# Cross-attention on one core: the order of the first projections, who rounds the key weights, and the warming matmuls

## The reference

```python
Q = (query @ Wq.T + bq)        # query x: (8, 112, 256); 16 heads of 16
K = (key_value @ Wk.T + bk)    # context: (8, 375, 256)
V = (key_value @ Wv.T + bv)
scores = einsum('bhqd,bhkd->bhqk', Q, K) / sqrt(16)
context = einsum('bhqk,bhkd->bhqd', softmax(scores), V)
x = context @ W_o.T + b_o + query
return (x - mean(x)) / sqrt(var(x) + 1e-5) * gamma + beta
```

## Time and profile before

| | us |
|---|---|
| median of 3 runs | 149.48 |
| the three runs | 149.48, 149.32, 150.67 |
| the profiled execution's own time | 148.18 |
| its span (first to last instruction) | 146.4 |
| outside the span in that execution | 1.78 |
| PE busy / DVE busy / ACT busy / POOL busy | 132.2 / 94.6 / 88.9 / 82.4 |

### The profile page before, as it was taken

How to read it: one execution, slowest core, us unless ns; L and a number is a source line. 1 busy time by engine, 2 the same in 40 slices (tenths; PEclk the granted TensorE clock), 3 DMA queues, 4 the chain that set the end, 5 groups by cost and what they waited for, 6 DMA issues and landing times.

```text
span 146.4 us, 3925 instructions
## 1 busy us (share of the span) xinstructions
PE 132.2 (90%) x1479; PEld 116.1 (79%) x1479; DVE 94.6 (65%) x223; ACT 88.9 (61%) x180; POOL 82.4 (56%) x101
## 2 busy tenths in 40 slices
PE   5799999799999789698999999999999999999950
PEld 4599778589799668588898989898989888878620
DVE  3446798797857745467657776877687787521532
ACT  3637734648587826647586678665867566787410
POOL 8963998394429441300429998991247006597441
PEclk9999999999999999999999999999999999999996
DMA  4985895584039999670007104651071000011111
GB/s 117 352 312 180 241 343 174 196 250 173 4 83 226 283 238 252 216 239 23 8 0 262 56 6 129 197 204 29 24 263 53 16 26 4 4 36 34 36 31 31
DMA packets 15731, 19.59 MB, mean 134 GB/s; under 512 B 2544, under 2 KB 14896, under 8 KB 15712
## 3 DMA queue, kind: packets, MB, share of 16 engines
q1 hardware_dynamic: 14656, 17.36, 37.2%
q0 software_dynamic: 592, 1.70, 4.7%
q10 hardware_dynamic: 464, 0.28, 0.6%
HBM read 6.30 MB, written 0.92 MB: 49 GB/s over the span
## 4 chain that ended last, share of the span: by engine, by line
PE 65%; SPq 13%; DMA 12%; DVE 3%; issue 2%; ACT 2%; ACTq 1%; POOLq 0%; DVEq 0%
PE m_bank L860 15%; PE pv_bank L952 13%; PE st_bank L934 12%; PE mx_bank L901 11%; SPq L269 6%; SPq L321 5%; PE m_bank L983 4%; DMA q_stack<-shift 4%; DMA k_stack<-k_hl 3%; DMA c_raw<-ctxT 3%; PE m_bank L963 2%; PE mx_bank L934 2%; DMA q_stack<-q_hl 2%; DVE mx L717 1%; SPq L354 1%
## 5 line engine op out<-in xcount | busy, mean ns | idle before, releaser
L717 DVE TENSOR_REDUCE mx<-mx_bank 112x1 f32<-112x375 f32 x128 | 64.1, 541 | 24.5 <-PE mx_bank L901 24.2
L617 ACT ACTIVATE pw<-st_bank 125x448 f32<-125x448 f32 x86 | 45.5, 544 | 23.0 <-PE st_bank L934 22.6
L901 PE MATMUL mx_bank<-k_stack,q_stack 128*112 128x376 f32 x128 | 43.8, 354 | 3.2 <-DMA k_stack<-k_hl 1.7
L934 PE MATMUL st_bank<-q_stack,k_stack 128*125 128x224 f32 x172 | 35.0, 285 | 2.0 <-DMA q_stack<-shift 1.4
L934 PEld LDWEIGHTS st_bank<-q_stack,k_stack 128*125 128x125 f32 x172 | 28.6, 186 | 5.4 <-issue 2.0
L901 PEld LDWEIGHTS mx_bank<-k_stack,q_stack 128*112 128x112 f32 x128 | 22.2, 176 | 6.4 <-issue 1.9
L421 POOL TENSOR_TENSOR k_hl<-k_full,k_hl 128x376 fp32r<-128x376 f32 x10 | 10.0, 1005 | 21.6 <-ACT k_hl L538 21.6
L952 PE MATMUL pv_bank<-pw,v_sb 125*17 125x112 f32 x744 | 21.7, 260 | 0.0
L395 POOL TENSOR_TENSOR c_hl<-c_raw,c_hl 128x752 fp32r<-128x752 f32 x6 | 10.9, 1810 | 16.2 <-ACT c_hl L509 16.2
L860 PE MATMUL m_bank<-c_hl,w_hl 128*128 128x376 f32 x84 | 18.5, 362 | 1.1 <-ACT w_hl L501 0.8
L952 PEld LDWEIGHTS pv_bank<-pw,v_sb 125*17 125x17 f32 x744 | 16.6, 97 | 3.2 <-issue 1.9
(11 more groups left out here) (111 smaller groups left out, 171.5 us busy)
## 6 DMA issues: line engine op xcount, KB each, us to landing
k_stack<-k_hl SPq DMA_DIRECT2D x48, 188.0 KB, 2.5
c_raw<-ctxT SPq DMA_DIRECT2D x8, 375.0 KB, 4.1
q_stack<-q_hl SPq DMA_DIRECT2D x12, 112.0 KB, 2.3
q_stack<-q_hl SPq DMA_DIRECT2D x6, 168.0 KB, 3.4
x_space<-x_nat POOLq DMA_DIRECT2D x1, 896.0 KB, 11.0
out<-yo SPq DMA_DIRECT2D x8, 112.0 KB, 2.0
pw<-wT SPq DMA_DIRECT2D x2, 256.0 KB, 4.6
x_space<-xT SPq DMA_DIRECT2D x2, 224.0 KB, 5.5
```

The lines of the kernel that those rows point to most:

```text
L617: nc.scalar.activation(p_tile[0:KC, n % PR, :, :], st_of(n)[0:KC, 0:4 * Q].rearrange("p (j q) -> p j q", j=4), ACT.Exp, scale=float(DK) ** ...
L717: nc.vector.tensor_reduce(mx[b % 2][:, h % 2, q_pair(h // 2):q_pair(h // 2) + 1], mx_bank[n % MR][0:Q, 0:KV], axis=AX_X, op=ALU.max, negat ...
L901: nc.tensor.matmul(mx_bank[n % MR][0:Q, 0:KVP], q_stack[k][:, side, q_pair(h // 2), b - Q_STACKS[k][0], :], k_stack[b % 3][:, h // 2, :], ...
L934: last = nc.tensor.matmul(st_of(n)[0:KC, k * 2 * Q:(k + 1) * 2 * Q], k_stack[i % 3][:, 2 * g + k, c * KC:(c + 1) * KC], q_stack[qk][:, :, ...
```

## The change

- **W_K is rounded by DVE** (`wk_hi_part`, a `tensor_copy`), ahead of the lo part of context 0, while ACT rounds context 0. ACT no longer does it. The lo part of W_K is made in two halves (`wk_lo_part(t)`, 256 elements a partition each). Semaphores `wk_hi` and `wk_lo` are new; `W_ORDER` is gone.
- **K of batch 0 by products** (`k_project_first`): both halves t get the first product, then both the second, then t = 0 the third and t = 1 the third. The number of matmuls is the same, 12.
- **The second Q group in front of K of batch 1**: the two `q_project(1, t)` leave `EARLY_JOBS` and stand between V of batch 0 and K of batch 1 on PE; ACT and DVE do their Q parts in the same order, x 1 is rounded ahead of context 1 and is loaded ahead of it. Banks: Q of group 1 goes to the S banks and K of batch 1 to the M banks. The remaining `EARLY_JOBS` move up by one or two heads.
- **Stacking**: side 0 of group 1 is issued by SP ahead of K of batch 1 (`stack_q(sp, 1, 0)`), side 1 by POOL behind its memset of the stack (`stack_q(pool, 1, 1)`).
- **DVE's early order**: `q_lo_part(1, t)` stands ahead of the early heads, `k_lo_part(2, 1)` behind head 15 and no longer behind head 16, `k_lo_part(2, 0)` behind head 13, the first half of the shift behind head 8 and no longer behind head 9.
- **ACT's early order**: both `v_part(1, n)` go ahead of rounding x 2, and x 3 is rounded behind the issue of the shift's half.
- **Warming**: one more float32 matmul, of 128 columns, behind the four.

```diff
--- before.py
+++ after.py
@@ -60,15 +60,14 @@
 
 
 EARLY_HEADS = 16
-EARLY_JOBS = {1: ("Q", 1, 0), 3: ("Q", 1, 1), 5: ("V", 1, 0), 7: ("V", 1, 1), 9: ("MT", 0, 0), 10: ("V", 1, 2),
-              13: ("K", 2, 0), 15: ("K", 2, 1)}
+EARLY_JOBS = {1: ("V", 1, 0), 3: ("V", 1, 1), 5: ("V", 1, 2), 8: ("MT", 0, 0), 11: ("K", 2, 0), 13: ("K", 2, 1)}
 FIRST_JOBS = {1: (("MT", 0, 1),), 5: (("Q", 2, 0),), 6: (("Q", 2, 1),)}
 
 
-S0_JOBS = [("Q", 0, 0), ("K", 1, 0), ("V", 1, 0), ("MT", 0, 0)]
-S1_JOBS = [("Q", 0, 1), ("K", 1, 1), ("V", 1, 1)]
-M0_JOBS = [("K", 0, 0), ("V", 0, 0), ("Q", 1, 0), ("K", 2, 0), ("V", 2, 0), ("Q", 2, 0), ("K", 3, 0)]
-M1_JOBS = [("K", 0, 1), ("V", 0, 1), ("Q", 1, 1), ("K", 2, 1), ("MT", 0, 1), ("V", 2, 1), ("Q", 2, 1), ("MT", 1), ("K", 3, 1)]
+S0_JOBS = [("Q", 0, 0), ("Q", 1, 0), ("V", 1, 0), ("MT", 0, 0)]
+S1_JOBS = [("Q", 0, 1), ("Q", 1, 1), ("V", 1, 1)]
+M0_JOBS = [("K", 0, 0), ("V", 0, 0), ("K", 1, 0), ("K", 2, 0), ("V", 2, 0), ("Q", 2, 0), ("K", 3, 0)]
+M1_JOBS = [("K", 0, 1), ("V", 0, 1), ("K", 1, 1), ("K", 2, 1), ("MT", 0, 1), ("V", 2, 1), ("Q", 2, 1), ("MT", 1), ("K", 3, 1)]
 for _i in range(1, B - V_AHEAD):
     if _i == 2:
         M1_JOBS.append(("BIAS",))
@@ -170,7 +169,7 @@
         shift_in = [sem(f"shift_in{i}") for i in range(2)]
         half_in = [sem(f"half_in{t}") for t in range(2)]
         stored = [sem(f"stored{i}") for i in range(2)]
-        w_hi, w_lo, wv_lo, x_hi, x_lo = sem("w_hi"), sem("w_lo"), sem("wv_lo"), sem("x_hi"), sem("x_lo")
+        wk_hi, wk_lo, w_hi, w_lo, wv_lo, x_hi, x_lo = sem("wk_hi"), sem("wk_lo"), sem("w_hi"), sem("w_lo"), sem("wv_lo"), sem("x_hi"), sem("x_lo")
         c_hi, c_lo, c_pad = sem("c_hi"), sem("c_lo"), sem("c_pad")
         ident_clear, ident_ready = sem("ident_clear"), sem("ident_ready")
         pv_clear = sem("pv_clear")
@@ -194,7 +193,6 @@
         last_scaled, last_ready = sem("last_scaled"), sem("last_ready")
         rstd_ready, y_ready, y_scaled, yo_ready = sem("rstd_ready"), sem("y_ready"), sem("y_scaled"), sem("yo_ready")
 
-        W_ORDER = (1, 0, 2)
         WIDE = UNITS * (B - 2) + 4
         LATE = WIDE + 2
         SINGLE = UNITS * (B - 2) + NC
@@ -302,8 +300,8 @@
             load_x(0)
             load_w(0)
             load_w(2)
+            load_x(1)
             load_context(1)
-            load_x(1)
             load_x(2)
             load_x(3)
             load_context(2)
@@ -334,12 +332,11 @@
             stack_q(sp, 0, 0)
             stack_k(0, 1)
             load_context(3)
+            stack_q(sp, 1, 0)
             for t in range(2):
                 stack_k(1, t)
-            stack_q(sp, 1, 0)
             sp.wait_ge(shift_ready, 1)
             stack_shift_half(sp, 0, 1)
-            stack_q(sp, 1, 1)
             for t in range(2):
                 stack_k(2, t)
             load_context(4)
@@ -379,7 +376,7 @@
             nc.gpsimd.memset(k_stack[0][:].bitcast(F32), 1.0).then_inc(k_ones[0], 1)
             nc.gpsimd.memset(k_stack[1][:].bitcast(F32), 1.0).then_inc(k_ones[1], 1)
             at = slice(2 * D, 3 * D)
-            pool.wait_ge(w_hi, W_ORDER.index(2) + 1)
+            pool.wait_ge(w_hi, 2)
             nc.gpsimd.tensor_tensor(w_hl[1][:, :, at], w_raw[:, :, at], w_hl[0][:, :, at].bitcast(F32),
                                     op=ALU.subtract).then_inc(wv_lo, 1)
             nc.gpsimd.memset(ident[:, :], 0.0).then_inc(ident_clear, 1)
@@ -389,6 +386,7 @@
             nc.gpsimd.memset(minus_half[:, :], -0.5).then_inc(half_ready, 1)
             stack_q(pool, 0, 1)
             nc.gpsimd.memset(q_stack[1][:].bitcast(F32), 0.0).then_inc(q_clear[1], 1)
+            stack_q(pool, 1, 1)
 
             def context_lo(b):
                 pool.wait_ge(c_hi, b + 1)
@@ -550,7 +548,6 @@
                                ).then_inc(v_ready, 1)
 
             context_hi(0)
-            w_hi_part(1)
             x_hi_part(0)
             w_hi_part(0)
             w_hi_part(2)
@@ -559,26 +556,27 @@
                 k_hi_part(0, t)
             for t in range(2):
                 q_hi_part(0, t)
+            x_hi_part(1)
             context_hi(1)
             for n in range(2):
                 v_part(0, n)
-            x_hi_part(1)
+            for t in range(2):
+                q_hi_part(1, t)
             for t in range(2):
                 k_hi_part(1, t)
             context_hi(2)
-            for t in range(2):
-                q_hi_part(1, t)
-            v_part(1, 0)
-            for k in range(2, NQ):
-                x_hi_part(k)
+            for n in range(2):
+                v_part(1, n)
+            x_hi_part(2)
 
             act.wait_ge(shift_hi, 1)
             stack_shift_half(act, 0, 0)
-            v_part(1, 1)
+            x_hi_part(3)
             for t in range(2):
                 k_hi_part(2, t)
             context_hi(3)
-            act.wait_ge(w_lo, 2)
+            act.wait_ge(wk_lo, 2)
+            act.wait_ge(w_lo, 1)
             act.wait_ge(wv_lo, 1)
 
             def take_o(b):
@@ -661,10 +659,20 @@
                 nc.vector.tensor_tensor(x_hl[:, 1, :, at], x_raw[:, :, at], x_hl[:, 0, :, at].bitcast(F32),
                                         op=ALU.subtract).then_inc(x_lo, 1)
 
-            def w_lo_part(k):
-                dve.wait_ge(w_hi, W_ORDER.index(k) + 1)
-                at = slice(k * D, (k + 1) * D)
+            def wk_hi_part():
+                dve.wait_ge(w_in[1], 16)
+                nc.vector.tensor_copy(w_hl[0][:, :, D:2 * D], w_raw[:, :, D:2 * D]).then_inc(wk_hi, 1)
+
+            def wk_lo_part(t):
+
+                dve.wait_ge(wk_hi, 1)
+                at = slice(D + t * PART, D + (t + 1) * PART)
                 nc.vector.tensor_tensor(w_hl[1][:, :, at], w_raw[:, :, at], w_hl[0][:, :, at].bitcast(F32),
+                                        op=ALU.subtract).then_inc(wk_lo, 1)
+
+            def wq_lo_part():
+                dve.wait_ge(w_hi, 1)
+                nc.vector.tensor_tensor(w_hl[1][:, :, 0:D], w_raw[:, :, 0:D], w_hl[0][:, :, 0:D].bitcast(F32),
                                         op=ALU.subtract).then_inc(w_lo, 1)
 
             def context_lo(b):
@@ -695,19 +703,23 @@
                 dve.wait_ge(const_in, 48)
                 nc.vector.tensor_tensor(bo_rows[:, :], src[0:Q, 0:D], bo_rows[:, :], op=ALU.add).then_inc(bias_ready, 1)
 
+            wk_hi_part()
             context_lo(0)
-            w_lo_part(1)
+            for t in range(2):
+                wk_lo_part(t)
             x_lo_part(0)
-            w_lo_part(0)
+            wq_lo_part()
             dve.wait_ge(bqk_in, 16)
             for t in range(2):
                 k_lo_part(0, t)
             for t in range(2):
                 q_lo_part(0, t)
+            x_lo_part(1)
             context_lo(1)
             for i in range(1, VR):
                 nc.vector.memset(v_sb[i][:, :, :, DK:VW], 1.0).then_inc(v_ones, 1)
-            x_lo_part(1)
+            for t in range(2):
+                q_lo_part(1, t)
             for t in range(2):
                 k_lo_part(1, t)
 
@@ -761,20 +773,18 @@
 
             for n in range(EARLY_HEADS):
                 head_max(n)
-                if n - 4 in range(2):
-                    q_lo_part(1, n - 4)
-                if n == H // 2 + 1:
+                if n == H // 2:
                     take_shift_half(0)
-                if n == 14:
+                if n == 13:
                     k_lo_part(2, 0)
+                if n == 15:
+                    k_lo_part(2, 1)
             for i in range(B):
                 for u in range(UNITS):
                     heads = MAX_HEADS[UNITS * i + u]
                     for n in heads[:1]:
                         head_max(n)
 
-                    if u == 0 and i == 0:
-                        k_lo_part(2, 1)
                     if u == 1 and i == 0:
                         take_shift_half(1)
                     if u in (6, 7) and i == 0:
@@ -861,20 +871,34 @@
                                                 stop=(k == len(PRODUCTS) - 1 and e == EC - 1))
                 return last
 
-            def w_split(k):
-                return W_ORDER.index(k) + 1
-
             def q_project(k, t):
                 dst, full = claim("Q", k, t)
                 project(dst[:, 0:q_width(k)], lambda a, e: w_hl[a][:, e, t * PART:(t + 1) * PART],
                         lambda a, e: x_hl[:, a, e, q_rows(k)],
-                        ((x_hi, k + 1), (w_hi, w_split(0))), (x_lo, k + 1), (w_lo, w_split(0))).then_inc(full, 1)
+                        ((x_hi, k + 1), (w_hi, 1)), (x_lo, k + 1), (w_lo, 1)).then_inc(full, 1)
 
             def k_project(b, t):
                 dst, full = claim("K", b, t)
                 project(dst[:, 0:KVP], lambda a, e: w_hl[a][:, e, D + t * PART:D + (t + 1) * PART],
                         lambda a, e: c_hl[b % 2][:, a, e, :],
-                        ((c_hi, b + 1), (w_hi, w_split(1))), (c_lo, b + 1), (w_lo, w_split(1))).then_inc(full, 1)
```

(28 more changed lines are left out.)

## The result

The changed kernel is slower. Its median is 152.04 us (151.02 to 154.16, 4 runs), that of the kernel before in the same call 149.40 us (148.69 to 150.67, 4 runs); the ratio is 1.030 (95%: 1.021 to 1.039). The forecast was 147.7 us.

The account below looks back on a forecast made before the run. PE was taken as the bound from 61 us on, the front before it as SP's DMA queue and DVE's list. 149.48 - 1.2 (front) - 0.6 (later clock rise in timed runs) = 147.7 us; range 146.4 to 149.5.

Parts of the forecast that it names:

- W_K is then rounded at 5.8: Start of PE: W_K lands at about 5.13, DVE's rounding takes at most 0.68 us, so K starts at 6.0, 0.4 earlier.
- The clock: PE, K of batch 0: hole closed, rise to 2.4 GHz at 7.7 (5.6 to 9.9), K ending 1.44 us earlier.
- rival 3: Front: Q ahead delays K(1) and DVE's list, with the clock's rise at 10.5 or later; 150.4 us, chance 0.07.
- rival 1: Front: the clock rises at once, moving the mark by 2.0 us; 146.7 us, chance 0.20.
- 0.6 us for a later rise in the timed runs: Timed runs above the profiled one: part is a later clock rise, which the change removes; 0.6 us, between 0 and 1.3.
- Q of group 1 ahead of K(1): PE's front: 1.46 us more ahead of K(1), cancelled by the earlier K; DVE's first maximum stays at 17.3.
- DVE's list: DVE to the shift's second-half rounding at 29.62: -0.72 (Q parts), -0.62 (gap), +0.15 (V jobs), -1.2 us in all.
- Queues: SP and POOL in the front: nine SP issues of 0.64 us put the shift's row at about 22.6, before 23.31.
- It's covered by the K part on DVE: PE's unit 0, behind the shift's row, moves from 26.85 to 26.2; DVE's K part hides it.
- Both of these hang on the maxima and shifts that come before them, so an earlier front moves them along: PE's DMA waits before 61 us, 1.7 us for batch 3's K stack and 1.4 for a shift, move with the front.
- rival 2: Warming fails (rise at 9.9, 0.2 us left) or the gain is lost behind 40 us (some 0.5 left); 149.1 us, chance 0.28.
- Slower: Whole kernel: chance 0.03 of being slower beyond 1%, above 151.0 us; 0.44 within 1%, 0.53 faster.

Follow-up runs that it names:

- e1: Changed kernel with POOL's memset of the second K stack moved behind W_V's lo part; 148.13 us against 148.57 before, ratio 1.001.
- e3: Changed kernel with DVE's copy of W_K written as a two-operand maximum of W_K with itself; 148.58 us, ratio to the kernel before 0.997.
- e5: Kernel before with only DVE's copy of W_K, ahead of context 0's lo part; 153.53 us against 148.36, ratio 1.036.
- e11: Kernel before with only one more warming matmul of 128 columns; 149.92 us, ratio 1.005.
- e4: Changed kernel with six warming matmuls of 256 columns in place of four, copy still held; 150.15 us, ratio to the kernel before 1.015.
- e13: Kernel before with all six of POOL's late loads issued near 34 us, ahead of the batch loop; 149.14 us against 148.83, ratio 0.993.
- e9: Kernel before with POOL's load of x in natural layout issued one batch later; 146.59 us against 148.76, ratio 0.986.
- e7: e3 with the second row of the shift's first half issued by ACT, not SP; 147.44 us against 148.36 before, ratio 1.000.
- e14: e3 with all of POOL's late loads issued near 34 us; 146.02 us against 148.83 before, ratio 0.989.
- e6: Changed kernel with W_K rounded by ACT, K of batch 0 one half after the other, no added warming matmul; 150.38 us, ratio to before 1.012.
- e8: e7 with POOL's load of x in natural layout issued one batch later; 145.55 us against 148.36 before, ratio 0.990.
- e16: e14 with the shift's second row issued by ACT; 150.51 us (5 runs) against 148.83 before, no ratio given.
- e2: Changed kernel with W_K rounded by ACT behind the context, as in the kernel before; 148.07 us, ratio to before 1.003.
- e12: e3 with POOL's load of x in natural layout issued one batch later; 148.13 us against 148.76 before, ratio 0.994.
- e15: e11 with all of POOL's late loads issued near 34 us; 148.99 us against 148.83 before, ratio 0.998.

## Why the prediction was wrong

- **The failed step: "W_K is then rounded at 5.8".** It rested on 0.68 us for the copy, called the upper end because DVE has no copy of that size in the trace before. Bounds from the nearest rows on DVE held only for DVE alone. The memset on POOL was in the timeline of before, from 4.8 to 7.4, over the very moment; that another engine could hold the copy to its end wasn't weighed. Measured: 0.43 us unheld, 2.57 held. It sent K's start to 7.83 for the forecast 6.0; with the hold away it is at 5.72 and 6.04. Shown by e1, e3 and e5.
- **The clock.** The prediction had the rise between 5.6 and 9.9, on the ground that the hole would be closed and that the hole was what had cost the rise. The late copy made the hole 1.80 us, and the rise came near 17.7, outside these bounds and outside rival 3's 10.5. Where the hole is closed or small (e1, e3, e11), K takes 2.40 to 2.62 us at full speed: rival 1's term, a rise at once, and right under its condition. e4 shows that the low clock is what the rest of the delay of K(1) is made of. That the hole was the cause in the kernel before isn't shown: e13 has the same front and the rise at once, so the 1.44 us that were to be won at K are won in some executions without the change. The rule cited from the Trainium skill, page "TensorE: Matmul & The Clock Gate", section "What's actually happening", that the rise differs from run to run, weighed more than I gave it: these profiles have it ahead of K, near 10.0, 11.5, 17.7 and 19.3.
- **0.6 us for a later rise in the timed runs.** No run shows one: the three profiles of the kernel before's front (before, e9, e13) have it near 10.0 or at once. The distance of 1.3 us between the profiled execution and the median was in part the three runs' own, as later medians of the kernel before are 148.36 to 148.83.
- **Q of group 1 ahead of K(1).** Priced at 1.46 us more ahead of K(1); measured 19.14 - 17.81 = 1.33. Right, and covered by the fast K in e1 and e3: K(1) at 13.04 and 13.12, first maximum at 16.43 and 16.52 for 17.29 before. The forecast had 17.3.
- **DVE's list.** -1.2 us at the mark was the forecast with the rise at 7.7, -2.0 with the rise at once. With the hold away and the rise at once, e3 has 27.92: -1.7. About right, with the gain partly spent on the shift's row. Luck has a part in it: K at full speed alone puts the mark at 28.61 in e13, 1.0 us early with nothing of the change in the front.
- **Queues.** The shift's row was forecast at 22.6, from 0.64 us an issue; in e3 SP needed 0.94 us for each of K(1)'s six and the row went at 23.89. "It's covered by the K part on DVE" was wrong by the 1.61 us that PE waited.
- **"Both of these hang on the maxima and shifts that come before them, so an earlier front moves them along."** This fails too, and by itself it would have cost the forecast: e1, e3, e7 and e11 have marks 0.8 to 2.2 us early and ratios of 0.997 to 1.005, and e11's wait grew from 1.7 us to 5.2. Why is in part open: longer waits in some profiles and a clock that falls more often are measured, their cause isn't. That is rival 2's second half, "the front's gain is lost again behind 40 us", at 0.28 in one with another cause. Its time of 149.1 us would have been right for the change without the hold. It deserved more than half of the chance, since the first wait of the earlier trace rows stands in a stretch with a DMA share of 1.05 (50 to 52 us of the kernel before), and the shift's transfers behind the second were issued into one of 1.04 (54 to 58), which I hadn't looked at.
- **Slower.** Rival 3 named the right direction and the right clock, but reached it through Q's order. The chance of 0.03 for slower was far too low: no case priced W_K's rounding above its upper end.

## What to carry to other kernels

When an instruction moves to VectorE, look at what GpSimd runs at that moment: an fp32 copy of one source from SBUF to SBUF waits for a running memset's end (0.43 us became 2.57), while a two-operand form of the same work (0.69 us) runs beside it. Beside GpSimd's own subtraction a two-operand instruction was held as well (1.75 us for 0.68), so the form helps only against the memset. An upper bound from one engine's rows is none if another engine can hold the instruction. And before pricing an earlier front, look for the first stretch where the DMA engines are full: a gain that arrives there may come out as a longer wait (e11), and a long wait may cost clock on top; moving other transfers (e9, and e14 on the changed kernel) was followed by a shorter time, shortening the front alone (e1, e3, e11) was not. And a fast stretch of PE in one profile is no property of the kernel: the same front ran at either clock.

## What the runs showed of the hardware

- DVE's copy and POOL's memset: 2.57 and 2.56 us beside it, 2.59 in e4, 0.43 without. DVE's two-operand subtraction: 0.68 us beside the memset, 1.75 beside POOL's two-operand subtraction.
- With 3.8 to 4.2 us of warming, PE reached full speed by or soon behind the start of K (e1 to e3, e6 to e8, e11 to e16), near 10.0 (before, e9), near 17.7 (after) or near 19.3 (e5); in the last two K started at 7.83. PEclk reads 1.00 in all of the first 28 us of the kernel after, while its weight loads show 330 ns up to V.
- After a wait of PE the granted clock went down to 0.50 and stayed under 1.00 for 3 to 8 us (after, e2, e4, e5, e6, e7, e11, e12, e14, e15, e16); in e3 it stayed at 1.00 behind 3.0 us and in e13 behind 2.6. In e2 it fell behind 2.5 us, and earlier behind 2.4.
- The six DMAs of one K stack took 6.6 to 10.2 us from the first issue to PE's release, over the 14 profiles that have this wait, in no order with the front.
